# An audio layer pipelined over tiles: weight preparations of the first two slots cut in pieces and placed elsewhere, with another order of work for the first two tiles

## What is computed

```python
h = dilated_attention(x)              # segments of 256, every second row: tiles of 128 rows
h = h + holographic(layernorm(h))     # circular convolution, decayed scan, circular correlation, gate
xf = layernorm(h)
idx, w = top2(softmax(gelu(xf @ rw1 + b) @ rw2 + b))        # router, 8 experts
v, z = 0, xf
for _ in range(2):
    ctx = concat(z, v)
    shared = gelu(ctx @ s_w1 + b) @ s_w2 + b                # 3*D control columns
    expert_k = gelu(ctx @ e_w1[k] + b) @ e_w2[k] + b        # two experts of eight
    # each: v' = sigmoid(a)*v - softplus(b)*(z - mu);  z' = z + 0.1*sigmoid(g)*v'
    # mixed with the shared weight and w, moved by a halting gate
refined = gelu(z @ r_w1 + b) @ r_w2 + b
out = h + xf + integration_weight * refined
```

## Time and profile before

| | |
|---|---|
| median of 3 runs | 765.87 us (765.49 to 766.56) |
| the profiled execution, own time | 766.59 us |
| its span, first to last instruction | 764.8 us |
| mean granted TensorE clock | 0.976 |
| busy: PE, PEld | 724.5 us (95%), 615.4 us (80%) |
| busy: DVE, ACT, POOL | 626.5 us (82%), 598.1 us (78%), 377.8 us (49%) |

### The profile page before, as it was taken

How to read it: one execution, slowest core, us unless ns; L and a number is a source line. 1 busy time by engine, 2 the same in 40 slices (tenths; PEclk the granted TensorE clock), 3 DMA queues, 4 the chain that set the end, 5 groups by cost and what they waited for, 6 DMA issues and landing times.

```text
span 764.8 us, 14327 instructions
## 1 busy us (share of the span) xinstructions
PE 724.5 (95%) x4516; PEld 615.4 (80%) x4516; DVE 626.5 (82%) x1430; ACT 598.1 (78%) x1382; POOL 377.8 (49%) x438
## 2 busy tenths in 40 slices
PE   5667999999999999999999999999999999999976
PEld 3446788888888888888888888887988888887876
DVE  3857788988988988988988988988889889888762
ACT  4765778788788788888888878888888888776672
POOL 1426456555555555555645545555555564563210
PEclk9888999999999999999999999999999999999995
DMA  8300000000000000000000000000000000000000
GB/s 330 124 15 1 8 1 17 6 22 8 15 22 1 21 21 3 20 23 1 22 22 1 22 21 1 21 22 1 21 21 1 8 8 2 8 9 1 8 8 14
DMA packets 11611, 17.27 MB, mean 23 GB/s; under 512 B 1232, under 2 KB 10504, under 8 KB 11024
## 3 DMA queue, kind: packets, MB, share of 16 engines
q1 hardware_dynamic: 11536, 16.35, 6.3%
HBM read 13.20 MB, written 3.15 MB: 21 GB/s over the span
## 4 chain that ended last, share of the span: by engine, by line
PE 89%; DVE 4%; ACT 3%; issue 2%; POOL 1%; DMA 1%; SPq 0%; ACTq 0%; POOLq 0%; DVEq 0%
PE ctl L495 23%; PE ctl L511 11%; PE ctl L472 5%; PE ctl L501 4%; PE ctl L514 4%; PE cd L593 4%; PE pa L593 4%; PE cd L472 3%; PE cd L666 3%; PE ctl L562 3%; PE ctl L481 2%; PE pa L588 2%; PE cd L588 2%; PE pb L593 2%; PE ctl L482 2%
## 5 line engine op out<-in xcount | busy, mean ns | idle before, releaser
L375 POOL TENSOR_TENSOR hm_lo<-gl,mexp 128x256 fp32r<-128x256 f32 x144 | 128.1, 914 | 100.0 <-DVE gl L1257 96.5
L495 PE MATMUL ctl<-w2e_hi,hm_hi 128*128 128x512 f32 (+1 forms) x432 | 158.6, 376 | 0.1
L495 PE MATMUL ctl<-w2e_lo,hm_hi 128*128 128x512 f32 (+1 forms) x432 | 150.8, 362 | 0.0
L495 PEld LDWEIGHTS ctl<-w2e_hi,hm_hi 128*128 128x128 f32 x432 | 82.2, 190 | 22.2 <-DVE hm_hi L1243 7.9
L511 PE MATMUL ctl<-w2e_hi,hm_lo 128*128 128x512 f32 (+1 forms) x432 | 99.9, 357 | 0.0
L1243 DVE TENSOR_TENSOR hm_hi<-ge,mexp 128x256 fp32r<-128x256 f32 x144 | 89.2, 634 | 12.4 <-ACT ge L946 9.4
L965 ACT ACTIVATE work<-ctl 128x256 f32<-128x256 f32 (+1 forms) x144 | 69.6, 484 | 35.4 <-PE ctl L514 27.4
L495 PEld LDWEIGHTS ctl<-w2e_lo,hm_hi 128*128 128x128 f32 x432 | 82.4, 191 | 10.6
L511 PEld LDWEIGHTS ctl<-w2e_hi,hm_lo 128*128 128x128 f32 x432 | 74.6, 188 | 13.7 <-POOL hm_lo L375 0.3
L381 POOL TENSOR_TENSOR rg_lo<-rg,rg_hi 128x512 fp32r<-128x512 f32 x23 | 33.2, 1445 | 74.9 <-ACT rg_hi L902 74.8
L917 ACT ACT_TABLE_LOAD x49 | 62.9, 1283 | 0.9
(11 more groups left out here) (210 smaller groups left out, 2061.4 us busy)
## 6 DMA issues: line engine op xcount, KB each, us to landing
work<-params_dram SPq DMA_DIRECT2D x3, 1152.0 KB, 12.6
xT<-turned_dram SPq DMA_DIRECT2D x24, 128.0 KB, 2.2
out_dram<-y SPq DMA_DIRECT2D x24, 128.0 KB, 1.7
xa<-x_dram SPq DMA_DIRECT2D x16, 128.0 KB, 2.3
par<-params_dram SPq DMA_DIRECT2D x1, 1280.0 KB, 10.3
work<-params_dram SPq DMA_DIRECT2D x2, 512.0 KB, 10.9
xa<-x_dram SPq DMA_DIRECT2D x8, 119.0 KB
par<-params_dram SPq DMA_DIRECT2D x1, 512.0 KB, 15.7
```

The source lines that it names most:

```text
L375: TT(hm[1][:, j, c, :], gl[:, c, part, :], pairs(tile, j, c), ALU.mult).then_inc(done, 1)
L495: mm(dst[:, a:z], hm[0][:, j, c, :], w2e[i][:, c, a:z], start=(c == 0 and i == 0), stop=False)
```

## The change

- w2a is copied in three pieces in slot -1 (`sides_weight`): ahead of the gelus of the expert layer, behind them, and behind eT.
- The low part of w2e is made in three pieces: two where it was, one behind the statistics of the next tile.
- In slots -1 and 0 the low part of the gelus and w3 (`first_halves`) move behind the first mask product, so the statistics of the next tile come ahead of them. w2b's last piece moves from the end of slot -1 behind the scans of slot 0.
- In the same two slots mexp is copied (`spread`) ahead of the exponential and its table load.
- r2 is scaled on VectorE in slot 0 (`refine_weight`); its low part is made by GpSimd in slot 1, in two pieces (`refine_weight_low`).
- The softplus of tile 0 moves from ahead of the shared units to behind mexp, without a reload of gelu's table behind it. Its `gated` moves to slot 1, behind the end rows, and its `weighted` in slot 1 behind xf.
- Waits on `set_pool` count one less.

```diff
--- before.py
+++ after.py
@@ -380,6 +380,16 @@
+            def refine_weight_low(k):
+
+                pool.wait_ge(set_dve, 5)
+                pool.wait_ge(set_act, 6)
+                r2m = staged("r2").rearrange("p (k c m) -> p k c m", k=2, c=REF // P // 2)
+                c = slice(2 * k, 2 * k + 2)
+                last = TT(r2[1][:, c, :], r2m[:, k, :, :], r2[0][:, c, :].bitcast(fp32), ALU.subtract)
+                if k == 1:
+                    last.then_inc(set_pool, 1)
+
             def state_lo(tile, part, src, hi_sb, done, joint):
 
                 passed(pool, hi_sb, tile)
@@ -423,6 +433,9 @@
 
                     passed(pool, x1_v, n)
                     TT(vu[n.s][:, 1, :], x1[n.s][:, :], pv("mu"), ALU.subtract).then_inc(u1_g, 1)
+                if t.low == 1:
+                    refine_weight_low(0)
+                    refine_weight_low(1)
                 if n.exists():
                     after = (u1_ps, -1) if t.exists() else (u2_ps, 1)
                     for j in range(2):
@@ -438,16 +451,6 @@
                     TT(vpe1[:, :], mv1[:, 1:2], eps_t[:, :], ALU.add).then_inc(vpe1_g, 1)
                     passed(pool, vpe1_g, e)
                     TT(rs1[:, :], vpe1[:, :], mhalf_t[:, :], ALU.pow).then_inc(rs1_g, 1)
-                if t.low == 0:
-
-                    pool.wait_ge(stage_in[4], 16)
-                    r2m = staged("r2").rearrange("p (c m) -> p c m", c=REF // P)
-                    TT(r2m, r2m, pv("iw").unsqueeze(1).to_broadcast([P, REF // P, D]), ALU.mult).then_inc(set_pool, 1)
-                    pool.wait_ge(set_pool, 3)
-                    pool.wait_ge(set_act, 6)
-                    TT(r2[1][:, :, :].rearrange("p c m -> p (c m)"), staged("r2"),
-                       r2[0][:, :, :].rearrange("p c m -> p (c m)").bitcast(fp32), ALU.subtract).then_inc(set_pool, 1)
-
             run(slot)
 
 
...
@@ -878,6 +881,23 @@
                 AF(w1s_x[0][:, :, :, :], w1s[:, 0:KD, :, :], ACT.Copy)
                 AF(w1e_x[0][:, :, :, :], w1e[:, 0:KD, :, :], ACT.Copy).then_inc(set_act, 1)
 
+            def sides_weight(k):
+
+                if k == 0:
+                    act.wait_ge(stage_in[3], 16)
+                last = AF(w2a[:, k, :], staged("w2a").rearrange("p (k m) -> p k m", k=3)[:, k, :], ACT.Copy)
+                if k == 2:
+                    last.then_inc(set_act, 1)
+
+            def spread(f):
+
+                passed(act, en2_v, f, back=NS, per=2)
+                passed(act, hl2_g, f, back=NS, per=3)
+                for i, (lo, hi) in enumerate(((0, 4), (4, 8))):
+                    passed(act, me_ps, f, per=2, step=i + 1)
+                    AF(mexp[f.s][:, lo:hi, :].rearrange("p c m -> p (c m)"), cd[:, lo * P:hi * P],
+                       ACT.Copy).then_inc(me_sb, 1)
+
             def routed_weight():
 
                 act.wait_ge(stage_in[5], 16)
...
@@ -1054,7 +1074,7 @@
                     if f.exists():
                         state_hi(0, pc, n, x1h_sb, f)
 
-                if t.exists():
+                if t.exists() and t.low > 0:
                     softplus_of(m, t)
                     table_of_gelus()
 
@@ -1069,7 +1089,11 @@
                         passed(act, gl1_v, t)
                     if m.exists():
                         passed(act, gl2_v, m)
+                    if f.low == 0:
+                        sides_weight(0)
                     expert_units(n.exists(), f.exists(), f)
+                    if f.low == 0:
+                        sides_weight(1)
 
                 if n.exists() and t.exists():
                     hi_part(n, 0, f, gh2_sb, gl2_v)
@@ -1078,6 +1102,8 @@
                     passed(act, eT_ps, e)
                     passed(act, att_ps, e, back=1)
                     AF(eT[:, :], pc[:, 0:P], ACT.Copy).then_inc(eT_sb, 1)
+                if f.low == 0:
+                    sides_weight(2)
 
                 if n.exists():
                     passed(act, pq1_v, n)
@@ -1113,7 +1139,11 @@
                     hi_part(f, 1, f, gh1_sb, gl1_v)
                     passed(act, dif_v, f)
                     AF(tw[:, :], dif[:, :], ACT.Tanh, scale=0.5).then_inc(tw_sb, 1)
-
+                    if f.low < 2:
+                        spread(f)
+
+                if t.low == 0:
+                    softplus_of(m, t)
                 if z.exists():
                     softmaxed(z)
                     if z.low == 0:
@@ -1129,18 +1159,10 @@
                     expert_units(True, False, f.at(1))
                     hi_part(t, 0, f.at(1), gh2_sb, gl2_v)
 
-                if f.exists():
-                    passed(act, en2_v, f, back=NS, per=2)
-                    passed(act, hl2_g, f, back=NS, per=3)
-                    for i, (lo, hi) in enumerate(((0, 4), (4, 8))):
-                        passed(act, me_ps, f, per=2, step=i + 1)
-                        AF(mexp[f.s][:, lo:hi, :].rearrange("p c m -> p (c m)"), cd[:, lo * P:hi * P],
-                           ACT.Copy).then_inc(me_sb, 1)
-                    if f.low == 0:
-
-                        act.wait_ge(stage_in[3], 16)
-                        AF(w2a[:, :, :].rearrange("p c m -> p (c m)"), staged("w2a"), ACT.Copy).then_inc(set_act, 1)
-                        first_weight()
+                if f.exists() and f.low > 1:
+                    spread(f)
+                if f.low == 0:
+                    first_weight()
 
                 if t.newest() or m.exists() and not n.exists():
                     passed(act, rl1_ps, m, back=1)
@@ -1150,7 +1172,7 @@
 
                 if t.low == 0:
 
-                    act.wait_ge(set_pool, 3)
+                    act.wait_ge(set_dve, 5)
                     AF(r2[0][:, :, :].rearrange("p c m -> p (c m)"), staged("r2"), ACT.Copy).then_inc(set_act, 1)
 
             run(slot)
@@ -1223,11 +1245,20 @@
                 V.tensor_tensor(w1e_x[1][:, :, :, :], w1e[:, 0:KD, :, :], w1e_x[0][:, :, :, :].bitcast(fp32),
                                 ALU.subtract).then_inc(set_dve, 1)
 
-            def routed_weight_low():
+            def refine_weight():
+
+                dve.wait_ge(stage_in[4], 16)
+                r2m = staged("r2").rearrange("p (c m) -> p c m", c=REF // P)
+                V.tensor_tensor(r2m, r2m, pv("iw").unsqueeze(1).to_broadcast([P, REF // P, D]),
+                                ALU.mult).then_inc(set_dve, 1)
+
+            def routed_weight_low(k):
 
                 dve.wait_ge(set_act, 3)
-                flat = [w[:, :, :].rearrange("p c m -> p (c m)") for w in w2e]
-                V.tensor_tensor(flat[1], staged("w2e"), flat[0].bitcast(fp32), ALU.subtract).then_inc(set_dve, 1)
+                last = V.tensor_tensor(w2e[1][:, k, :], staged("w2e").rearrange("p (k m) -> p k m", k=PC)[:, k, :],
+                                       w2e[0][:, k, :].bitcast(fp32), ALU.subtract)
+                if k == PC - 1:
+                    last.then_inc(set_dve, 1)
 
             def shared_lo(tile, s_sb, sh, sab, done):
 
@@ -1256,6 +1287,14 @@
                 passed(dve, read, tile, back=1, per=3)
                 V.tensor_tensor(gl[:, :, part, :], ge[:, :, part, :], gh[:, :, part, :].bitcast(fp32),
                                 ALU.subtract).then_inc(gl_v, 1)
+
+            def first_halves(f):
+
+                part_lo(f, 1, gh1_sb, gl1_v, hl1_g)
+                passed(dve, tw_sb, f)
+                V.tensor_scalar(w3[f.s][:, 1:2], tw[:, :], homsw, homsw, ALU.mult, ALU.add)
+                V.tensor_scalar(w3[f.s][:, 2:3], tw[:, :], nomsw, homsw, ALU.mult, ALU.add).then_inc(w3_v, 1)
+                passed(dve, w3_v, f)
 
             def last_refine_lo(o):
 
...
@@ -1352,11 +1391,15 @@
                     if f.low == 0:
                         gated_mix()
 
+                if t.low == 0:
+                    shared_weight_low(range(2, 3)).then_inc(set_dve, 1)
                 if t.exists():
                     last_ps, back = (u2_ps, 2) if m.exists() else (u1_ps, 1)
                     mask_hi(t, 1, 1, t, hm1_v, last_ps, back)
                     for j in range(2):
                         end_lo(t, j, 1, gl1_v, hm1_v, en1_v)
+                if n.low == 0 and t.exists():
+                    gated(n)
 
                 if f.exists():
                     passed(dve, retr_ps, f)
@@ -1367,7 +1410,7 @@
                     passed(dve, rs2_g, f, back=1)
                     V.bn_aggr(mv2[:, :], st[:, :]).then_inc(mv2_v, 1)
 
-                if n.exists() and t.exists():
+                if n.exists() and t.exists() and n.low > 0:
                     weighted(n)
 
                 if f.exists():
@@ -1382,6 +1425,8 @@
                         first_weight_low()
 
                 if n.exists() and t.exists():
+                    if n.low == 0:
+                        weighted(n)
                     moved(n)
 
                 if m.exists() and not last_in:
@@ -1451,23 +1496,25 @@
                     part_lo(n, 0, gh2_sb, gl2_v, hl2_g)
                     for j in range(2):
```

(26 more changed lines are left out.)

## The result

The changed kernel takes 758.43 us (median of 4 executions, 757.62 to 759.14) against 766.12 us (4 executions, 765.49 to 766.56): a ratio of 0.9902, 95% interval 0.9889 to 0.9914. The forecast was 757.7. The number came out nearly right, and part of that is luck: in the two traced executions the first slots gained 4.8 us, not 8.3, and the end of the kernel gained 3.2 us, which the prediction did not have.

A forecast was written before the change was run, and what follows sets the result against it. TensorE was taken to bound the kernel from 72.16 us on. Slot 1's first transpose came 8.8 us sooner, its joint layer 8.3; 766.6 - 8.3 = 758.3, 0.7 above the median: 757.6, stated as 757.7, range 756.7 to 759.2.

The forecast's parts named there:

- Translation from 72.16 on: From slot 1's joint layer to the end, nothing changes but the earlier start: 692.6 us as before.
- Rival 1: Clock falls again in slot 1, joint layer pays 2.0 us or twice that: 759.7, up to 761.7; chance 0.2.
- Slot -1, 1.84 us: With w2a and w2e_lo in thirds, statistics start at 29.67 and xn comes at 31.25, 1.84 us sooner.
- the last third "beside GpSimd's rsqrt": In slot -1, w2e_lo's last third runs behind bn_stats beside GpSimd's rsqrt; xn still comes 1.58 us after bn_stats.
- h2 of slot 0 at 37.8: Slot 0: VectorE is last and h2 comes at 37.8, 2.4 us sooner; TensorE is ready at 37.2.
- 4.8 us taken for TensorE's piece: Slot 0: TensorE's piece up to h2's matmul starts at 32.4 and takes the same 4.8 us, until 37.2.
- Softplus, 2.3 us: Slot 0: without softplus ahead of the shared units, the transposition waiting for ge comes 2.3 us sooner.
- r2's scaling, 1.2 us: End of slot 0: scaling r2, 1024 columns, on VectorE takes 1.2 us, from 47.2 to 48.4.
- xn without its neighbour, 2.0 us: Slot 0 to slot 1: xn without GpSimd's r2 scaling beside it takes 0.41 instead of 2.42 us.
- Slot 1: Gives some back: TensorE waits 1.2 us for x1, joint layer comes at 63.9 against 72.16, 8.3 us sooner.
- GpSimd's low pieces at nothing: Slot 1: r2's two low pieces on GpSimd could cost 0 to 2.4 us; taken as 0, by a 4.24 us gap.
- Rival 2: VectorE has more to do than counted, 1.5 to 3.5 us given back, 759.2 to 761.2; chance 0.12.

The follow-up runs named there:

- before_tail: Kernel before the change with 41 extra identity matmuls in waits of its last three slots: 763.63 us, ratio 0.9986.
- before_tuned: Kernel before the change with 14, 8, 2 and 5 calls of filler matmuls in its last slots only: 762.84 us, ratio 0.9965.
- after_softplus: Changed kernel with tile 0's softplus and its two table loads back ahead of the shared units, gated back in slot 0: 758.67 us.
- tuned2: tuned with r2's scaling moved into VectorE's router wait in slot 0 and tile 0's weighted split around xf: 754.86 us, ratio 0.9856.
- r2_tail: Changed kernel with 41 extra matmuls at its end, r2's scaling and low part back on GpSimd at slot 0's end: 759.52 us.
- after_start: Changed kernel with fill(9) filler matmuls ahead of x1's turn in slot 1 and fill(5) ahead of the joint layer: 759.55 us.
- tuned: Changed kernel with filler calls, 5 and 2 in slot 1 and 14, 8, 2 and 5 at the end: 754.75 us, ratio 0.9875.

## Why the prediction was right, and where it was not

The changes of place worked by the waits that the prediction named, and several steps gained less than forecast. The number was met because the end, which the forecast had put at nothing, made up for it; that is luck.

- **Translation from 72.16 on**: from the end of the joint layer to the turn of x2 it was right, to 0.02 us over 660 us. "The rest of the kernel is a translation" failed at both edges: in the joint layer (Rival 1, below) and in the last stretch. It left out that the end has waits in which the clock falls, and that in the trace of before it had stayed low there, at 0.59 over 23 us. A translation of the work isn't one of the clock. In the traced pair the 3.2 us made up for the 3.4 by which the start-up fell short (4.84 against 8.26).
- **Slot -1, 1.84 us**: it was 0.34. Of the missing 1.5 us, 0.9 lie ahead of the statistics. VectorE's w2e_lo started at 28.81, not at 27.95, as it stood behind the scores, and TensorE's layer and scores ran slower (four score matmuls in 1.06 us instead of 0.61). In before_tail and before_tuned, which are unchanged there, they took 1.06 us too, so this differs between executions and isn't the change's. The other 0.6 us is the last third "beside GpSimd's rsqrt": taken at nothing, it cost 0.6 us (vpe 0.81 instead of 0.19).
- **h2 of slot 0 at 37.8**: 39.07, late by 1.3 of the 1.5 us by which xn was late. VectorE was last, as said, but only by 0.16 us (its end rows ended at 39.03, TensorE's matmul of the retrieval at 38.87). The 4.8 us taken for TensorE's piece were 5.3, as the retrieval now ran at half clock (1.75 us instead of 1.23).
- **Softplus, 2.3 us**: the transposition that waits for ge came 3.3 us sooner, 1.1 of it from before and 2.2 of its own. By the trace that is right, and again the table load takes 1.28 us and softplus starts 0.02 us behind it (51.82, 53.12). In the time it was worth 0.2 us, for the reason that after_softplus shows.
- **r2's scaling, 1.2 us**: 1.64, with GpSimd's base sums beside it (48.29 to 49.07); alone in tuned2 it took 1.22. The Trainium skill (GPSIMD Engine Reference, Key points) states contention between GpSimd and VectorE's instructions with two SBUF inputs, and I had applied it to the base sums only. Here VectorE's scaling was slowed and the sums were not (0.72 to 0.78 us); in the kernel before, the last sum took 1.44 us beside gated. So either side can lose.
- **xn without its neighbour, 2.0 us**: right, 0.41 instead of 2.42, and r2_tail brings the 2.43 back.
- **Slot 1**: the wait for x1 was forecast at 1.2 us and is 1.37. The joint layer came at 65.75 instead of 63.9. Of these 1.85 us, 1.7 are carried over from the terms above and 0.2 are vu's, which took 0.91 us instead of 0.75 beside GpSimd's xj_lo.
- **GpSimd's low pieces at nothing**: right. They run from 70.44 us in the joint layer, and at full clock it takes 5.85 to 5.90 us with them and 5.83 to 5.86 without.
- **Rival 1** (the clock falls once more, chance 0.2, 2.0 us) happened, with 1.57 us. The forecast called the stretches ahead denser; from 62.60 to 64.03 TensorE had 0.06 us of work.
- **Rival 2** (VectorE has more to do than counted, 1.5 to 3.5 us, chance 0.12) happened in part: vpe 0.6, r2's scaling 0.4 and vu 0.2 make 1.2 us. Without the gain at the end, which it doesn't know of, the time would lie in or near its 759.2 to 761.2.

## What to carry to other kernels

Where TensorE is slowed by its clock after a wait, microseconds saved ahead of the wait don't add up. Of four parts undone alone, three lost 1.6 to 2.3 us less in the time than they delayed the dense layer, and some 1.5 us of that is the clock, which then held in the layer. Read the granted clock at the kernel's end as well as at its start before calling the rest a translation, and sum a change's gain up to a mark that both kernels pass at the same clock. Trace each kernel more than once before splitting a gain of 1% into shares: here one share changed by 1 us from one pair of traces to the next. Filler matmuls paid here only where they were shorter than the wait that they filled; behind a fall they ran at half speed (2.21 us instead of 1.38), and where the wait had shrunk they were what was waited for (tuned2, after_start).

## What the runs showed of the hardware

- With the same instructions the last stretch took 23.19 us at a granted clock of 0.59 (before), 21.19 at 0.76 (after_start) and 20.01 at 0.83 (after). With fillers of fitting size it took 18.40 to 18.45 at 1.00 (before_tuned, tuned).
- The clock differs between executions of one start-up. In before_tail the granted clock falls at 16.8 and rises at 27.0 us, and the scores of slot -1, at 26 us, took 1.06 us; in the trace of after the row reads 1.00 from the start to 31 us and they took 1.06 as well; in that of before it reads 1.00 and they took 0.61. Ahead of its first change the clock's row thus doesn't tell which clock there was.
- A GpSimd addition of one column took 0.81 us beside a VectorE subtraction of 768 columns with two SBUF inputs (after) and 0.19 when alone (before). Two of VectorE's end rows took 3.19 us beside a GpSimd subtraction 1024 wide (r2_tail) and 0.60 without it (after).
